# Later 4-head self attentions: loads of queries and keys asked for at the old stack's last scores, maximum products begun one tile sooner

## The reference, cut to what matters

```python
Q = relu(q @ Wq + bq); K = relu(k @ Wk + bk); V = relu(v @ Wv + bv)      # 4 heads of 64 features
scores = einsum('hbqd,hbkd->hbqk', Qh, Kh) / sqrt(64)
scores = where(key_mask == 0, NEG, scores)
attn   = softmax(scores) * query_mask
out    = einsum('hbqk,hbkd->hbqd', attn, Vh) + q
enc    = layer_norm(out, gamma, beta)        # then leaky_relu(enc @ Wff + bff) + enc
```

## Time and profile before

| | us |
|---|---|
| median of 3 runs | 1555.49 |
| lowest, highest | 1551.62, 1557.13 |
| the profiled execution | 1554.63 |
| its span, first to last instruction | 1552.9 |

### The profile page before, as it was taken

One profiled execution on the slowest core, in us unless ns is written; L12 is line 12 of the kernel. 1 busy time (PEld: TensorE's weight loads), 2 busy tenths in 40 slices (PEclk: granted clock), 3 DMA queues, 4 the chain that ended last, 5 costly groups with the idle time before them and its releaser, 6 DMA issues.

```text
span 1552.9 us, 21719 instructions
## 1 busy us (share of the span) xinstructions
PE 1338.1 (86%) x7242; PEld 768.5 (49%) x7242; DVE 1071.0 (69%) x2669; ACT 748.6 (48%) x1046; POOL 529.5 (34%) x447
## 2 busy tenths in 40 slices
PE   5868999998789979889998979799998788788897
PEld 4513333332278756544443346443443677545796
DVE  4677888887654267766567777675767888676654
ACT  5405556666777345623334445233443734345664
POOL 3001111111330042306876622168865257001212
PEclk9959999999989999989999999799999889899998
DMA  7952333320000000554422306714400020730001
GB/s 256 260 126 47 59 58 62 66 47 2 28 0 1 1 1 34 157 176 96 96 50 46 115 35 196 195 38 95 96 28 1 28 35 22 164 65 3 1 1 54
DMA packets 79864, 110.29 MB, mean 71 GB/s; under 512 B 16591, under 2 KB 55689, under 8 KB 77961
## 3 DMA queue, kind: packets, MB, share of 16 engines
q1 hardware_dynamic: 79753, 108.91, 28.3%
HBM read 70.55 MB, written 37.80 MB: 70 GB/s over the span
## 4 chain that ended last, share of the span: by engine, by line
PE 40%; POOLq 19%; DVE 16%; issue 11%; ACT 7%; DVEq 3%; SPq 2%; DMA 1%; POOL 1%; ACTq 0%
POOLq L1109 18%; PE banks L1220 6%; PE banks L1565 5%; PE banks L1580 5%; PE banks L1162 4%; PE banks L1195 3%; PE banks L2151 3%; DVE mask_rows L1390 2%; PE banks L2181 2%; DVE max_parts L1394 2%; DVE scratch L1390 1%; PE banks L1173 1%; DVE max_parts L1379 1%; ACT x_feat L1355 1%; PE banks L2699 1%
## 5 line engine op out<-in xcount | busy, mean ns | idle before, releaser
L1355 ACT ACTIVATE x_feat<-banks,key_bias 128x1024 f32<-128x1024 f32 x160 | 176.4, 1115 | 264.6 <-PE banks L1202 208.7
L1108 POOL TENSOR_TENSOR x_feat<-x_feat 128x1024 f32<-128x1024 f32 (+1 forms) x112 | 243.0, 2169 | 97.0 <-ACT x_feat L1355 88.6
L1162 PE MATMUL banks<-stacks 128*128 128x512 f32 (+4 forms) x640 | 229.2, 406 | 36.5 <-DVE max_parts L1383 12.7
L1220 PE MATMUL banks<-x_feat,v_group 128*32 128x512 f32 (+4 forms) x1312 | 231.3, 568 | 8.4 <-ACT x_feat L1355 4.8
L1355 ACT ACTIVATE x_feat<-banks 128x1024 f32<-128x1024 f32 (+2 forms) x224 | 178.8, 841 | 111.7 <-PE banks L1195 110.5
L1162 PEld LDWEIGHTS banks<-stacks 96*128 96x128 bf16 (+1 forms) x640 | 78.5, 139 | 223.9 <-DVE max_parts L1383 91.6
L1132 POOL TENSOR_SCALAR_AFFINE_SELECT x_feat<-x_feat 128x256 f32<-128x256 f32 x128 | 53.7, 422 | 281.3 <-ACT x_feat L1355 279.6
L1195 PE MATMUL banks<-stacks 99*128 99x512 bf16 (+3 forms) x512 | 129.9, 344 | 20.1 <-ACT x_feat L1355 13.7
L1383 DVE CUSTOM_DVE_ANT_0 scratch<-banks,mask_rows 128x512 f32<-128x512 f32 x128 | 88.3, 689 | 50.6 <-PE banks L1162 50.4
L1201 PE MATMUL banks<-stacks 128*128 128x512 f32 x256 | 111.0, 434 | 9.5 <-DMA stacks<-neg_max_parts_r 9.5
L1565 PE MATMUL banks<-stacks 128*128 128x512 f32 x384 | 102.2, 405 | 9.3 <-DVE stacks L1547 8.4
(11 more groups left out here) (301 smaller groups left out, 2465.0 us busy)
## 6 DMA issues: line engine op xcount, KB each, us to landing
stacks<-q_parts_r SPq DMA_DIRECT2D x18, 512.0 KB, 11.9
stacks<-k_parts_r SPq DMA_DIRECT2D x18, 512.0 KB, 13.7
q_parts_r<-stacks SPq DMA_DIRECT2D x16, 512.0 KB, 3.2
k_parts_r<-stacks SPq DMA_DIRECT2D x16, 512.0 KB, 3.4
v_group<-v SPq DMA_DIRECT2D x14, 512.0 KB, 14.8
stacks<-q_parts SPq DMA_DIRECT2D x16, 384.0 KB, 5.0
w_even<-in_w SPq DMA_DIRECT2D x4, 1024.0 KB, 6.6
stacks<-q_parts SPq DMA_DIRECT2D x16, 256.0 KB, 5.4
```

The source lines that it names most:

```text
L1108: e.tensor_tensor(total, total, p, ALU.add)
L1162: m = e.matmul(PS[:, bank, at:at + wide], q[0:rows, h, qt * P:(qt + 1) * P], keys[0:rows, h, k0:k0 + wide], start=True, stop=True, skip_gr ...
L1220: m = e.matmul(PS[w * h:w * (h + 1), bank, t.q0:CH], V[:, h, :], PB[:, t.index % 2, h // 2, h % 2, 0:CH - t.q0], start=t.first, stop=t.las ...
L1355: e.activation(dst, PS[:, 2 * (st % 2):2 * (st % 2) + 2, 0:CH - t.q0], ACT.Exp, scale=A.scale, bias=bias).then_inc(s.p_ready, 1)
```

## The change

The line in `order` lets the maximum products of stacks 1 and 2 begin in step 4. They are then 32 products in nine steps: 4, 4, 3, 4, 3, 4, 3, 4, 3 in steps 4 to 12. In `attention_sync` the loads of queries and keys, pieces 0 to 2, are asked for when the old stack's last scores are done; the values, piece 3, wait for the value products as before. The causal attention and the last block keep their order.

```diff
-        start = 5 if A.self and A.dh == 64 else 0
+        start = 4 if A.self and A.dh == 64 else 0
...
             if g < A.n:
+                if A.halved:
+                    need(e, s.s_ready, (g - A.slots + 1) * A.steps)
+                    load_group(e, A, g, slot_of(A, g), (0, 1, 2))
                 need(e, s.pv_tile, (g - A.slots + 1) * A.nt)
-                load_group(e, A, g, slot_of(A, g))
+                load_group(e, A, g, slot_of(A, g), (3,) if A.halved else (0, 1, 2, 3))
```

## The result

The changed kernel takes 1563.33 us (median of 13 runs, 1559.66 to 1571.32), the kernel before, run beside it, 1558.30 (13 runs, 1551.62 to 1566.89). The ratio is **1.0046**, with a 95% interval of 1.0031 to 1.0061: slower. The profiled execution took 1562.33 us, its span is 1560.6.

What follows compares the result with a forecast made beforehand. PE was taken to set the pace, standing some 3.7 us more in stack 2. Spreading -0.4, statistics +6.4, scales -0.8 and clock +4.0 gave +9.2 on 1554.63: 1563.8 us, own range 1559 to 1568, 8-in-10 range 1554 to 1569.

Steps and rivals of the forecast that it cites:

- the sum: Whole kernel: -0.4 + 6.4 - 0.8 + 4.0 = +9.2 us on the profiled execution's 1554.63, giving 1563.8.
- The load: SP's query and key loads for the next stack: start 1.57 us sooner, at about 803.53, after the maximum rows.
- its last part: Signs expected in the profile after: load times, key waits, a 2.7 us DVE wait in step 5, and stack lengths.
- The wait for keys: First product of each stack, now in tile 4: waits grow by 0.54 us, to about 2.1, 2.0, 1.0 and 0.5.
- Spreading: Products over steps 4 to 12 of stacks 1 and 2: -0.11 us per load-waiting stack, -0.4 over four.
- The statistics: Stack 2, DVE's second layer norm statistics behind four products: PE held, +3.2 us in each attention, +6.4 together.
- The scales: Stack 2, step 7: hold DVE as before, but step 8 waits for one product less, -0.4 us each, -0.8.
- The clock: PE's clock falls behind two statistics waits and two load waits of about 2 us: +4.0 us, bounds 0 to 6.
- The contention: DVE and POOL adds slow each other: each statistics would be 0.9 us longer, the sum 1.8 higher, near 1565.6.
- The prediction's sign: Stack 2 expected longer than its 55.0 us by 3 to 5; the prediction is wrong if it doesn't grow.
- wait for wait: Rival: load waits swap, clock holds, banks cover more of the statistics; +2.6 us or 1557, between 1554 and 1559; chance 0.25.
- Faster: Rival: loads land in under 11.7 us, so all four key waits go; 1550.4 us; chance 0.08.

Runs made afterwards that it cites:

- the early load alone: The changed kernel with its products beginning in step 5 again, so only the key and query loads come sooner; ratio to the kernel before 0.9960, in two comparisons.
- early start alone: The kernel before with the products beginning in step 4 instead of 5, loads as before; ratio to the kernel before 1.0085.
- without the second statistics: The changed kernel with the addition, variance and mean of the second four token tiles left out in stack 2; ratio to the kernel before 1.0012.
- the kernel without 1e-8: Early load with products from step 5, and the scales' first instruction, adding 1e-8 to the deviation, left out in stack 2; ratio to the kernel before 0.9965.
- statistics in step 3: The changed kernel with the second statistics of stack 2 moved from step 4 to step 3, before the first products; ratio to the kernel before 1.0042.
- neither statistics nor first scale: The changed kernel without the second statistics and without the scales' first instruction in stack 2; ratio to the kernel before 0.9959.

## Why the prediction was right, and where its terms were off

The time was right (1563.8 forecast, 1563.33 measured), and so were the sign and the main mechanism, the second statistics behind products. That the time fits to 0.5 us is luck. The rise of 9.2 us was put on an execution of 1554.63, while the kernel before has a median of 1558.30 over 13 runs; the medians differ by 5.0. By the ratio the rise is 7.2 us (4.8 to 9.5), and in the four stacks, where the sum has all of it, it is 3.3 and 4.6 in two profiles. So the base was about as much too low as the rise was too high. By its own steps:

- **The load.** Right by its working: it starts 0.04 us behind the rows and 0.74 behind the end of the last scores (803.97), where the working had 803.53 against 802.78. The 1.6 us behind that end, which its last part names, was a slip: 1.57 is how much sooner the load comes. Wrong was that the 3.5 us of waits for keys are all that an earlier load can take away: alone it shortens the four stacks by 5.8. Beside the keys it spared the clock, which doesn't fall at tile 8 then; PE's busy time in stack 2 goes from 49.65 and 49.68 to 48.00.
- **The wait for keys.** Mis-sized: 0.92, 0.54, 0.85 and 0.94 instead of 2.1, 2.0, 1.0 and 0.5, in the order of the prediction. The working kept each place's landing as it was in the one profile. From the first load's issue to the first product that waited, 13.77, 13.74 and 12.66 us had passed at the three places of the earlier trace rows; in the changed kernel it was 12.25 to 12.65 at all four. In the profiles of this study that show such a wait 20 of 27 places lie between 12.0 and 13.3 and 7 between 13.6 and 13.9, in the same kernel as well. The sign of it stood in the earlier trace rows: the third wait was 0.42 and not 1.5.
- **Spreading.** Right. In stack 1 of the first attention steps 6, 7 and 8 took 3.23, 3.06 and 3.20 us (first scores at 773.67, 776.90, 779.96, 783.16), where 3.21, 3.17 and 3.21 were worked out, and steps 9 to 12 together 15.38 (to 798.54), where it was 15.34. For the stack -0.11 was forecast if the keys land as before. Stack 1 of the second attention is 1.67 shorter; its keys landed 13.74 us behind their issue before and 12.25 now, 1.49 sooner, which leaves about -0.2.
- **The statistics.** Right: the sum has +3.2 for each (the last part of the prediction names a wait of some 2.7), and the waits are 3.32 and 3.40, behind exactly the instructions named. But what they cost isn't theirs alone. Taking them out recovers 0.25% (1.0037 to 1.0012; the intervals overlap) of the 0.77% that the start costs, since the scales then hold PE in their place.
- **The scales.** Mis-sized: -0.4 was forecast for each; the waits fell from 2.36 to 0.77 and from 1.72 to 0.75, 1.6 and 1.0. "The scales in step 7 hold DVE as before" was the step that failed: in the changed kernel they took 1.8 us (836.89 to 838.64), not 3.3 as before (829.61 to 832.94). Two meetings with POOL make most of the difference. The first scale came 1.71 us into POOL's add instead of 1.10 and so waited less for its end; and the third, of two inputs, met no instruction of POOL, where before it took 0.79 us. DVE and POOL before, then in the changed kernel:

```profile
829.61 1.31 DVE L414 TENSOR_SCALAR std<-std 128x4 f32<-128x4 f32 x1
...
831.60 0.79 DVE L421 SCALAR_TENSOR_TENSOR minus_mean_rstd<-mean_var,rstd 128x4 f32<-128x4 f32 x1 [0.43 <-issue]
```
```profile
828.51 2.38 POOL L1108 TENSOR_TENSOR x_feat<-x_feat 128x1024 f32<-128x1024 f32 x1 [1.53 <-ACT x_feat L1355]
```
```profile
836.89 0.71 DVE L414 TENSOR_SCALAR std<-std 128x4 f32<-128x4 f32 x1
...
837.93 0.16 DVE L421 SCALAR_TENSOR_TENSOR minus_mean_rstd<-mean_var,rstd 128x4 f32<-128x4 f32 x1
```
```profile
835.18 2.40 POOL L1111 TENSOR_TENSOR x_feat<-x_feat 128x1024 f32<-128x1024 f32 x1 [1.79 <-ACT x_feat L1358]
```

- **The clock.** Mis-sized, and the gain left out. The sum had four falls and +4.0. The two behind the statistics came, longer than assumed; none came behind the waits for keys; and the two falls of before at tile 8 went away with their waits, which the sum doesn't have. Busy PE in stack 2 shows the net: 49.70 to 50.41 in the first attention, +0.7 and not the 2 or so that the sum has for it. Against the early load alone, where the clock stays up, the fall costs 50.41 - 48.00 = 2.4 us.
- **The contention.** The prediction cited the Trainium skill, page "GPSIMD Engine Reference", section 8, for a contention of DVE with POOL, and its estimate from the earlier trace rows was 0.9 us more for each add. The adds took 1.97 and 2.05, so 0.5 and 0.6 more than 1.47. Nor was 1.47 free of POOL: with no POOL instruction beside it the add takes 1.23 us (early start alone, 821.80). What the contention does to the scales I hadn't looked at, and there it is larger: they take 3.3 us or 1.8.

In sum, stack 2 of the first attention: the long waits before products were 1.55 + 2.36 = 3.91 us and are 0.92 + 3.32 + 0.77 = 5.01, 1.1 more, and PE's busy time is 0.7 more; the stack is 1.55 longer, so some 0.3 of other idle time went. In the second attention it is 3.3 longer. The prediction's sign was 3 to 5, so the first attention missed it.

The rival "wait for wait" had the four stacks about right in this profile (+2.6 against +3.3), for another reason: the clock fell, and the scales gave it back. "Faster" needed the loads to land within 11.7 us; the fastest that made a product wait took 12.0. But the early load without the earlier start, which no rival considered, is the faster one: its products ask a tile later, 13.6 to 13.8 us behind the issue, and in its two profiles none of the eight had to wait.

## What to carry to other kernels

Price both parts of a change apart: here a gain of 0.4% was hidden under a loss of 0.8%, and the part that took the slack spent what the other had made. Before work is moved into a wait, see what already lies in it: DVE's layer norm did, and moving or cutting one piece of it only handed the hold to the next. A landing time isn't one number; take its spread from all places where the trace shows it.

## What the runs showed of the hardware

**Some of DVE's instructions wait for POOL's add, to its end.** The residual add on DVE ends 1.08 to 1.09 us behind the end of the POOL add that ran when it started, whatever its own length, in each of 47 places in thirteen profiles: 805.89 + 2.37 = 808.26 against 807.18, 815.61 + 1.47 = 817.08 against 815.99 in the kernel before; 823.36 against 822.27 in the changed one. With no POOL instruction beside it, it takes 1.20 to 1.23 us. The first scale, on 4 elements, ends 0.02 to 0.03 behind POOL's add: it is 1.90 us long without the second statistics, 1.31 in the kernel before, 0.71 in the changed kernel, where POOL was nearly done, and 0.16 when POOL isn't in an add. Not every instruction waits. In the kernel without 1e-8, DVE's reciprocal ran in 0.17 us in the middle of POOL's add, and the next instruction, with two inputs in SBUF, waited until 833.85, the add's end (831.45 + 2.38 = 833.83):

```profile
832.56 0.17 DVE L1305 RECIPROCAL rstd<-std 128x4 f32<-128x4 f32 x1
832.81 1.04 DVE L1307 SCALAR_TENSOR_TENSOR minus_mean_rstd<-mean_var,rstd 128x4 f32<-128x4 f32 x1
```
```profile
831.45 2.38 POOL L1111 TENSOR_TENSOR x_feat<-x_feat 128x1024 f32<-128x1024 f32 x1 [0.57 <-ACT x_feat L1362]
```

The Trainium skill, page "SBUF — State Buffer", section "Who interferes with whom", says that a DVE instruction with two SBUF inputs, or in a mode that uses both ports, contends with GpSimd, and that whichever issues first holds the shared ports while the other blocks. The adds and the last instruction agree with it. Whether the first scale, which reads one tensor, ran in such a mode, no run here shows. With another instruction of POOL, on one input, the rule doesn't fit the profile's spans, which are rough on POOL: the third scale of the kernel before ended at 831.60 + 0.79 = 832.39, 1.05 us behind the start of POOL's and 1.72 ahead of its end (831.34 + 2.77 = 834.11).

**The clock doesn't follow the length of a wait alone.** It fell to 0.50 behind waits of PE of 1.67 (1115.73, statistics in step 3), 1.92, 1.98, 2.11, 2.36 and 3.32 us. It stayed at 1.00 behind a wait of 2.35 us at tile 8 of the same stack in the kernel with the early load alone, behind one of 2.22 us for keys (1061.03) in the kernel with neither statistics nor first scale, and behind one of 2.80 us (835.09, statistics in step 3). What decides between them these runs don't show.
